# Rotary products of queries and keys: sine table repeated over four heads, two products in place of four

## What is computed

```python
q = (x @ Wq).reshape(b, n, N_HEADS, HEAD_DIM)          # x is the layer-normed input
k, v = jnp.split(ctx @ Wkv, 2, axis=-1)
# apply_axial_rope(q, pos), apply_axial_rope(k, pos):
freqs = ROPE_BASE ** (-jnp.arange(half) / half)         # half = 2
ang = pos[..., :, None] * freqs
cos, sin = jnp.cos(ang)[:, :, None], jnp.sin(ang)[:, :, None]
x1, x2 = (xr[..., 0], xr[..., 1])                       # neighbours of each pair
out = jnp.stack([x1 * cos - x2 * sin, x1 * sin + x2 * cos], axis=-1)
w = jax.nn.softmax(jnp.einsum('bqhd,bkhd->bhqk', q, k) * scale, axis=-1)
x = x + jnp.einsum('bhqk,bkhd->bqhd', w, v).reshape(b, n, 256) @ Wout + bout
x = x + ffn(layernorm(x))                               # the experts
```

## Time and profile before

| | |
|---|---|
| median of 3 runs | 539.51 us (539.47 to 539.99) |
| the profiled execution | 543.16 us |
| its span in the trace | 541.4 us |
| TensorE matmuls busy | 478.0 us (88%) |
| VectorE busy | 409.6 us (76%), 1263 instructions |
| ScalarE busy | 352.2 us (65%) |
| GpSimd busy | 364.9 us (67%) |
| sine products L729 | 27.9 us in 128 instructions |
| cosine products L721 | 22.1 us in 32 instructions |

### The profile page before, as it was taken

The page is one execution under the profiler, slowest core; times in us unless marked ns, Lnnn a source line. Parts: engine busy times, 40 slices in busy tenths (PEclk is TensorE's granted clock), DMA queues, the critical chain, the costliest instruction groups (busy, mean ns, idle before and its releaser), DMA issues.

```text
span 541.4 us, 21775 instructions
## 1 busy us (share of the span) xinstructions
PE 478.0 (88%) x7701; PEld 367.2 (68%) x7701; DVE 409.6 (76%) x1263; ACT 352.2 (65%) x929; POOL 364.9 (67%) x634
## 2 busy tenths in 40 slices
PE   3667899999999999999999998888969999998890
PEld 2544567666666766666676675568969999897780
DVE  7375489989899999999999889865725556776663
ACT  2472567777778777777877777666636666665550
POOL 4333467888888888888888887438726556665651
PEclk9996799999999999999999999999979999999986
DMA  7900001111121212212121101143543446778844
GB/s 198 262 24 17 18 18 52 41 59 54 48 73 49 83 60 68 63 48 65 38 73 41 58 25 34 54 117 112 187 117 119 121 134 201 234 231 259 279 137 157
DMA packets 43226, 54.56 MB, mean 101 GB/s; under 512 B 6727, under 2 KB 36849, under 8 KB 43122
## 3 DMA queue, kind: packets, MB, share of 16 engines
q1 hardware_dynamic: 36642, 36.32, 24.0%
q0 software_dynamic: 6480, 16.85, 8.6%
HBM read 29.60 MB, written 23.94 MB: 99 GB/s over the span
## 4 chain that ended last, share of the span: by engine, by line
PE 52%; DVE 25%; issue 9%; DMA 6%; SPq 3%; ACT 2%; POOL 2%; POOLq 0%; DVEq 0%
DVE negmax L744 12%; PE logit_banks L1514 9%; PE bank L1370 6%; PE logit_banks L1330 5%; PE qkv_banks L1279 5%; PE logit_banks L1533 5%; PE logit_banks L1338 4%; DVE ropes L729 4%; PE qkv_banks L1290 3%; PE qkv_banks L1270 3%; DMA y_in<-result_rows 3%; PE bank L1490 2%; DMA xres<-in_L_ffn_W_dram 2%; DVE rden L751 2%; PE qkv_banks L1320 1%
## 5 line engine op out<-in xcount | busy, mean ns | idle before, releaser
L675 POOL DMA_INDIRECT result_rows<-blocks_io,blk_dest x71 | 71.8, 1011 | 64.9 <-ACT blocks_io L1225 36.1
L641 POOL DMA_INDIRECT routed_rows<-xs,slots x64 | 65.8, 1029 | 16.9 <-issue 16.9
L744 DVE TENSOR_REDUCE negmax<-logit_banks 128x16 f32<-128x1024 f32 x64 | 75.0, 1212 | 2.7 <-PE logit_banks L1311 2.7
L1124 ACT ACTIVATE late<-logit_banks 128x1024 f32<-128x1024 f32 x64 | 62.0, 1021 | 17.2 <-PE logit_banks L1338 17.2
L648 POOL TENSOR_TENSOR ropes<-rope_a,ropes 128x512 f32<-128x512 f32 x32 | 41.2, 1286 | 38.3 <-DVE ropes L729 38.3
L1009 DVE TENSOR_TENSOR gated<-xn,logit_banks 128x176 f32<-128x176 f32 x71 | 23.8, 336 | 54.4 <-ACT xn L1231 54.3
L751 DVE RECIPROCAL rden<-bank 128x256 f32<-128x256 f32 x32 | 55.9, 1746 | 1.3 <-PE bank L1363 0.8
L1514 PE MATMUL logit_banks<-w_hi,x_hi 128*128 x142 | 48.2, 339 | 8.8 <-issue 5.7
L1231 ACT ACTIVATE xn<-logit_banks 128x176 f32<-128x176 f32 x71 | 22.5, 317 | 48.4 <-PE logit_banks L1514 48.4
L632 POOL TENSOR_TENSOR mid<-mid,mask 128x512 f32<-128x512 f32 x44 | 44.7, 1035 | 11.0 <-ACT mid L1105 11.0
L1514 PE MATMUL logit_banks<-w_hi,x_lo 128*128 x142 | 46.8, 329 | 0.0
(11 more groups left out here) (220 smaller groups left out, 1384.2 us busy)
## 6 DMA issues: line engine op xcount, KB each, us to landing
blocks_io<-routed_rows SPq DMA_DIRECT2D x71, 129.0 KB, 2.1
y_in<-result_rows SPq DMA_DIRECT2D x16, 512.0 KB, 5.3
x_sb<-in_x_dram SPq DMA_DIRECT2D x32, 128.0 KB, 2.0
out_dram<-o_sb SPq DMA_DIRECT2D x16, 256.0 KB, 5.6
ctx_sb<-in_ctx_dram SPq DMA_DIRECT2D x32, 64.0 KB, 2.0
blocks_io<-in_L_ffn_W_dram SPq DMA_DIRECT2D x4, 512.0 KB, 6.4
mid<-mT SPq DMA_DIRECT2D x128, 4.0 KB
routed_rows<-pad_row SPq DMA_DIRECT2D x15, 129.0 KB, 2.9
```

What stands on the lines that cost most here:

```text
L641: nc.gpsimd.indirect_dma_start(routed[:, :], bass.IndirectOffsetOnAxis(ap=slots[:, t.slot(TR), k:k + 1], axis=0), xs[:, t.slot(TR), k, :], ...
L675: nc.gpsimd.indirect_dma_start(results[:, :], bass.IndirectOffsetOnAxis(ap=blk_dest[:, b.slot(RB):b.slot(RB) + 1], axis=0), y_sb[:, b.slot ...
L744: V.tensor_reduce(negmax[:, t.par, 16 * half:16 * half + 16], ps_s[:, 1024 * half:1024 * half + 1024].rearrange("p (h k) -> p h k", k=N), ...
L1124: S.activation(pT[:, 1024 * half:1024 * half + 1024], ps_s[:, 1024 * half:1024 * half + 1024], ACT.Exp, scale=SCALE).then_inc(exp_done, 1)
```

## The change

The sine table holds its four values repeated for the four heads of a group, so that a tile's part is 2 x 4 x 4 values in place of 2 x 4; the two activations that write it read the angles repeated. In `rope`, one product for each of queries and keys takes both halves i: it writes the 256 columns in order and reads them with the two halves of each group in reversed order (a step of -16 elements over i). The four operations of 128 elements become two of 256. The order of the operations on every engine stays, and so do all waits.

```diff
-        sin_t = sb("sin_t", [P, T, 2, 4])
+        sin_t = sb("sin_t", [P, T, 2, GH, 4])
...
-                for i in range(2):
-                    sn = sin_t[:, t.n, i, :]
-                    o = rope_b.rearrange("p (x s i h c) -> p x s i h c", x=2, s=2 * RG, i=2, c=4)[:, :, :, i]
-                    q = qk.rearrange("p x (s i h c) -> p x s i h c", s=2 * RG, i=2, c=4)[:, :, :, 1 - i]
-                    for x in range(2):
-                        ins = V.tensor_tensor(
-                            o[:, x], q[:, x],
-                            sn.unsqueeze(1).unsqueeze(1).broadcast_to([P, 2 * RG, GH, 4]), ALU.mult)
+                sn = sin_t[:, t.n].rearrange("p i h c -> p i (h c)").unsqueeze(1).broadcast_to([P, 2 * RG, 2, 4 * GH])
+                o = rope_b.rearrange("p (x s i m) -> p x s i m", x=2, s=2 * RG, i=2)
+                for x in range(2):
+                    q = qk[:, x].rearrange("p (s i m) -> p s i m", s=2 * RG, i=2)[:, :, ::-1]
+                    ins = V.tensor_tensor(o[:, x], q, sn, ALU.mult)
                 ins.then_inc(rope_done, 1)
...
-                S.activation(sin_t[:, :, 0, :], af[:, 0], ACT.Sin, scale=-1.0).then_inc(rope_tables, 1)
-                S.activation(sin_t[:, :, 1, :], af[:, 0], ACT.Sin).then_inc(rope_tables, 1)
+                for i in range(2):
+                    S.activation(sin_t[:, :, i], af[:, 0].unsqueeze(2).broadcast_to([P, T, GH, 4]), ACT.Sin,
+                                 scale=2.0 * i - 1.0).then_inc(rope_tables, 1)
                 S.activation(cos_t[:], af[:, 1], ACT.Sin).then_inc(rope_tables, 1)
```

## The result

| | before | changed |
|---|---|---|
| median, same chip (20 runs each) | 540.05 us | 537.27 us |
| changed over before | | 0.9921 (95% interval 0.9901 to 0.9942) |
| the profiled execution | 543.16 us | 537.36 us |
| its span | 541.4 us | 535.6 us |
| VectorE busy, instructions | 409.6 us, 1263 | 404.8 us, 1199 |

The change is faster by 0.8%, which is 4.3 us on 540.05, with an interval of 3.1 to 5.3 us; the medians differ by 2.8 us. The ratio is of fast executions, without two of the changed kernel's twenty that lie more than 1.5% above its fastest (541.81 and 543.88 us); the means of all twenty differ by 3.2 us. The forecast was 2.9 us and 536.6 us, so the size of the gain lies just under the interval.

A forecast was written before the change was run, and what follows sets the result against it. TensorE and VectorE were taken to alternate on the chain, with 0.17 us of TensorE slack per tile. 26 turns at 0.11 us give 2.9 us, other terms nothing: 539.5 us falls to 536.6, range 535.0 to 539.7.

The forecast's parts named there:

- The bound, and the chain through the sine products: Attention loop: TensorE and VectorE take turns on the chain; the sine products have 0.87 us of each turn.
- 0.11 us per tile: Rotation: two sine products of 256 elements take 0.76 us against 0.87 for four of 128, saving 0.11 us.
- 26 turns of 29, the three tied ones giving nothing: Loop: 26 turns with 0.17 us TensorE slack gain 2.9 us; three turns with the chain on TensorE alone gain nothing.
- The reversed read at no charge: Sine products: reading the halves in reversed order costs nothing, like the broken order of L721's cosine operand.
- The tables hidden: Before the first tile: larger sine activations cost 0.34 us more, up to 0.85, hidden behind other waits; cost nothing.
- The later stages shift as a whole: After the loop: nothing in the later stages is touched; they start 2.9 us earlier, unchanged.
- a longer expert stage: Sign of a wrong prediction: a shorter loop together with a longer expert stage.
- Half of it: Rival, loop: TensorE has only 0.05 us to give, gain 1.3 us, 538.2 us; chance 0.10.
- Larger: Rival, sine products: a PSUM start costs over 0.06 us; TensorE caps gain at 0.17 per turn, 4.4 us, 535.1; chance 0.03.
- Nothing: Rival: gain given back in the expert stage, or access pattern costs 0.055 us per product; 539.5 us; chance 0.13.
- Slower by the reversed read: Rival, sine products: reversed halves read at half rate, 0.43 us more per turn, 12.5 us in all, 552.0; chance 0.03.

The follow-up runs named there:

- eight products: Kernel before with each sine product cut in two, eight of 64 elements per tile, against the kernel before: ratio 1.0183, 552.33 against 542.42 us.
- the run with one product: Changed kernel with the keys' sine product left out from the fourth tile on: ratio 1.0209 against the kernel before, 553.83 against 541.44 us.

## Why the prediction was right

*The bound, and the chain through the sine products.* Right. Twice the starts made every turn longer by what they cost, and half the starts made it shorter by as much.

*0.11 us per tile.* Right in mechanism, small by a sixth. The term was two products at 0.34 us from start to start, taken from a sum whose follower starts 0.34 us later. It measured 0.33, so the products give 0.13 us per turn. The other estimate in the text, from the line through 128 and 512 elements, had 0.12 and was nearer.

*26 turns of 29, the three tied ones giving nothing.* Wrong, and to the cautious side. The recorded idle time did fall from 0.17 to 0.04 us, as 0.17 - 0.13 says, but it is not TensorE's slack: by the starts that was 0.32 us and is 0.20 now. In the three turns called tied TensorE had lost 0.16 to 0.18 us in the attention's products, for a reason that the profile does not show, and was still in time. In the first profile of the changed kernel it lost as much in the same three turns, and they take 9.34, 9.37 and 9.34 us, after 9.47, 9.49 and 9.47: they gained like the others. At 0.13 us, 29 turns give 3.8 us. The 27 turns gained 3.2, 3.5 and 3.8 us in three profiles, of which 0.40 is the hold-up that moved out of the last one. Some turns gained less. In the first profile five are long (9.47 to 9.60 us), in the third only two, which are long in the kernel before as well. What TensorE loses between 0.20 and 0.32 us was covered before and is not now: of the 0.47 us lost in the turn of 9.60 us, 0.26 show.

*What the prediction did not look at.* The maxima also wait for the plain logits. That path had 0.15 us to give, the change took 0.13, and the fit is luck: the prediction names no such wait. A saving of 0.25 us per turn would have been cut short there, and not by TensorE's way to L1300.

*The reversed read at no charge.* Right: 415 against 414 ns. L721's cosine operand was a fair neighbour.

*The tables hidden.* Right: the two sine activations start at 11.08 and the cosine's at 12.13, so each costs 0.32 us more than its 0.20 before (forecast 0.34); the first L721 still waits for L1277 and starts at 12.90, against 12.78. Timeline of ScalarE and VectorE, changed kernel, to the earlier trace rows:

```profile
11.08 1.15 ACT L1160 ACTIVATE sin_t<-ang 128x512 f32<-128x512 f32 x2
12.13 0.29 ACT L1162 ACTIVATE cos_t<-ang 128x128 f32<-128x128 f32 x1
...
12.90 0.69 DVE L721 TENSOR_TENSOR rope_a<-qkv_banks,cos_t 128x512 f32<-128x512 f32 x1 [2.08 <-PE qkv_banks L1277]
```

*The later stages shift as a whole.* Not settled finely. After the loop the profiles take 212.1 us before and 214.5, 213.6 and 214.3 with the change, but also 215.2 with the four old products on the new table, and 212.6 with the two new ones in order. The prediction had named a longer expert stage as a sign against it, but the extra time lies ahead of the experts' main part. From the last L721 to the last inverted sums of the attention the kernel before takes 28.4 us and the changed one 32.1, 30.1 and 31.6; from there to the end it is 183.6 against 182.3, 183.4 and 182.6. With the old products that first stretch also took 30.0 (table alone) and 29.4 us (eight products), so no single profile can tell 2 us there, and whether the change has a share in it is open.

*The rivals.* Half of it: no, the loop alone has 2.7 us or more even without its last turn. Larger: its price of a start is refuted. Its number, 4.4 us, is near the measured ratio, but the loop shows 3.2 to 3.8, and what may be left of the 4.3 lies within the interval. Its cap of 0.17 us per turn was read from modelled ends; the cap of 0.15 that the traces show belongs to the plain logits. Nothing: no, three comparisons have their whole interval under 1. Slower by the reversed read: no. What a further cut of VectorE runs into was not on the list at all: a hold-up by GpSimd.

## What to carry to other kernels

Where two engines take turns on the chain, read three things: the price of a start (two sizes of the same operation, start to start, give it), every wait of the operation through which the turn is handed over (here the maxima, which need the plain logits besides VectorE's own queue), and the slack of the partner. Take that slack from starts, in the turns where the partner came late, and not from the idle time behind a modelled end: here the idle time said 0.17 us and the starts 0.32. A saving pays in full up to the smallest of these, 0.15 us here. Before cutting further, look at which operations of GpSimd lie beside VectorE's small operations with two operands in SBUF, since an engine that gets ahead can move them on top of each other.

## What was not expected of the hardware

A sum of 8 elements on VectorE took 0.97 us instead of 0.19, ending with GpSimd's operation beside it, and removing 0.33 us of VectorE's work per turn made the kernel 2.7% slower than the changed one on the same chip (553.83 against 539.13 us, by medians). Beside GpSimd's indirect DMA a sum took 0.77 us as well, but not every such sum did, and the cause is open.

The time before the loop came in two kinds. In the kernel before, the run with the halves in order and the run with one product, the second L721 of the loop starts at 72.9 to 73.4 us; in the ten others between 65.6 and 70.2. The window view of the kernel before, from 40 to 60 us, has

```profile
45.00:50.00 5.00, 3.58 (x15) 2.27 (x15) 2.10 (x4) 1.73 (x6) 2.72 (x3) 0.50 0.02 5
...
55.00:60.00 5.00, 4.17 (x50) 2.06 (x51) 1.29 (x3) 2.12 (x4) 3.41 (x5) 0.63 0.01 3
```

and the changed kernel has

```profile
45.00:50.00 5.00, 3.59 (x22) 2.45 (x22) 3.07 (x5) 1.73 (x6) 2.72 (x3) 0.84 0.01 4
...
55.00:60.00 5.00, 5.00 (x105) 2.88 (x93) 1.21 (x3) 4.61 (x11) 2.23 (x3) 1.00 0.02 5
```

In both kernels TensorE had stood idle for about half of the five microseconds before (2.68 of 5 us busy from 40 to 45 in the kernel before, 2.07 in the changed one), and in both the clock then fell to its lower level, 1.2 GHz (0.50 and 0.84 from 45 to 50 us). That alone does not make the start late: a second profile of the changed kernel has 0.50 there too and starts at 68.83. What the late ones have is a second fall. Between 55 and 60 us the kernel before has 0.63, after TensorE had waited 1.30 us for the maxima up to 55.83, the halves in order 0.64 and the one product 0.67; all three still have 0.65 to 0.69 from 60 to 65. The ten others have 1.00 from 55 to 60. Old and new products are in both groups. Two single profiles can thus differ by 5 us ahead of any line that a change touches.
